# The loop over the tiles beyond the fixed list, at the beginning of an edge pass instead of its end

## The reference

```
def _gnn_layer(edge_index, x, edge_attr, norm, We, be, Wn, bn):
    src, dst = (edge_index[0], edge_index[1])
    parts = [x[src], x[dst]]
    if edge_attr is not None:
        parts.append(edge_attr)
    e = jax.nn.relu(jnp.concatenate(parts, axis=-1) @ We + be)
    msg = e * norm[:, None] if norm is not None else e
    agg = jax.ops.segment_sum(msg, dst, num_segments=x.shape[0])
    x_new = jax.nn.relu(jnp.concatenate([x, agg], axis=-1) @ Wn + bn)
    return (x_new, e)
```

## Time and profile before

| | |
|---|---|
| median of 3 runs | 2377.35 us (2377.28 to 2377.51) |
| the profiled execution | 2376.61 us |
| its span | 2374.4 us |
| mean granted clock of TensorE in it | 0.914 |
| busy: PE, DVE, POOL, ACT | 2020.9, 1455.5, 1063.3, 662.9 us |
| edge pass 0, first POOL gather to node stage | 998.4 to 1412.3 |
| edge pass 1 | 1450.3 to 1884.7 |
| edge pass 2 | 1922.2 to 2335.5 |

### The profile page before, as it was taken

The page is one execution under the profiler, slowest core; times in us unless marked ns, Lnnn a source line. Parts: engine busy times, 40 slices in busy tenths (PEclk is TensorE's granted clock), DMA queues, the critical chain, the costliest instruction groups (busy, mean ns, idle before and its releaser), DMA issues. The chain is left out here.

```text
span 2374.4 us, 50364 instructions
## 1 busy us (share of the span) xinstructions
PE 2020.9 (85%) x14516; PEld 1445.6 (61%) x14516; DVE 1455.5 (61%) x4548; ACT 662.9 (28%) x1344; POOL 1063.3 (45%) x1086
## 2 busy tenths in 40 slices
PE   7687776999999997398888866999999769999983
PEld 4221113454544543287777755999999659888881
DVE  6888873132322323687878846767777467777774
ACT  0145663121211211332333324323233231111111
POOL 0444430000000000377777736777777267777770
PEclk7767767999999998699999978999999889999996
DMA  3022445000000001544444425777777345555541
GB/s 91 14 49 67 87 83 47 0 0 0 0 0 0 0 0 44 209 132 142 143 145 142 144 77 136 210 209 207 209 205 210 93 127 146 146 140 144 142 121 30
DMA packets 188937, 242.83 MB, mean 102 GB/s; under 512 B 53217, under 2 KB 115068, under 8 KB 188076
## 3 DMA queue, kind: packets, MB, share of 16 engines
q1 hardware_dynamic: 155420, 173.31, 25.4%
q0 software_dynamic: 32864, 60.32, 11.1%
q10 hardware_dynamic: 432, 6.29, 0.6%
HBM read 150.92 MB, written 69.26 MB: 93 GB/s over the span
## 5 line engine op out<-in xcount | busy, mean ns | idle before, releaser
L1504 POOL DMA_INDIRECT rows<-p_dram,src_i x912 | 893.0, 979 | 305.1 <-issue 257.4
L1737 DVE TENSOR_TENSOR agg_t<-psum,agg_t 128x128 f32 x1368 | 390.2, 285 | 153.2 <-PE psum L1621 122.9
L1603 PE MATMUL psum<-w_c,before 128*128 128x128 f32 x1824 | 403.6, 303 | 0.0
L1672 ACT ACTIVATE rows<-rows 128x512 f32<-128x512 f32 x228 | 143.7, 630 | 754.6 <-DVE rows L1730 750.5
L884 PE MATMUL psum<-adj,parts 128*128 (+2 forms) x1750 | 339.7, 351 | 5.6 <-ACT agg L963 4.4
L1721 DVE TENSOR_SCALAR hot_w<-col_f,dst_loc,weight 128x128 f32<-128x128 f32 x912 | 319.1, 354 | 0.3
L664 PE MATMUL psum<-src_hot,dst_hot 128*128 128x391 f16 x586 | 228.0, 432 | 81.3 <-ACT psum L686 27.5
L1603 PEld LDWEIGHTS psum<-w_c,before 128*128 128x128 f32 x1824 | 279.7, 194 | 0.0
L1264 POOL MEMSET agg_t<- 128x3200 f32 x1 | 2.8, 2766 | 606.5 <-POOLq L1020 606.5
L1621 PE MATMUL psum<-hot_w,rows 128*128 128x128 f32 x1824 | 247.3, 279 | 29.8 <-ACT rows L1672 25.8
L884 PEld LDWEIGHTS psum<-adj,parts 128*128 128x128 f16 x1750 | 153.0, 98 | 191.1 <-issue 23.4
(11 more groups left out here) (249 smaller groups left out, 2504.3 us busy)
## 6 DMA issues: line engine op xcount, KB each, us to landing
e_dram<-after SPq DMA_DIRECT2D x228, 256.0 KB
before<-e_dram SPq DMA_DIRECT2D x228, 256.0 KB
adj<-stage SPq DMA_DIRECT2D x196, 97.8 KB, 3.5
pair_rows<-sorted_rows SPq DMA_DIRECT2D x114, 128.0 KB, 4.3
rows<-p_dram,src_i POOLq DMA_INDIRECT x912
hot_all<-dst_rows SPq DMA_DIRECT2D x1, 3584.0 KB, 12.5
hot_all<-dst_rows ACTq DMA_DIRECT2D x1, 3072.0 KB, 17.3
hot_all<-dst_rows ACTq DMA_DIRECT2D x1, 2048.0 KB, 10.5
```

The costliest lines, as they stand in the source:

```text
L1504: nc.gpsimd.indirect_dma_start(out=rows[:, b % ROWS, m * D:(m + 1) * D], out_offset=None, in_=p_dram, in_offset=bass.IndirectOffsetOnAxis( ...
L1603: mm = nc.tensor.matmul(o, before[:, q % BEFORE, m * P:(m + 1) * P], w_c[:], start=False, stop=True)
L1672: nc.scalar.activation(e_of(q), source, ACT.Relu).then_inc(e_on, 1)
L1737: nc.vector.tensor_tensor(a, psum[:, A_BANKS[q % len(A_BANKS)], m * P:(m + 1) * P], a, ALU.add).then_inc(agg_on, 1)
```

## The change

The loop's code moves on every engine to the beginning of the pass. On DVE it comes behind the first pair and the twelve `hot_w` operations of the first three slots; on POOL, PE and ACT it comes first. On SP it comes behind the first loads and ahead of the next weights. The loop gets six buffers of its own. The first tile's records are loaded as the pass's first DMA, those of a following tile at the end of a round (so one load more than there are tiles). The sum's product goes to the last of the banks of A_BANKS, for which PE waits at the third slot until the first ordinary sum has been taken (`agg_on`). The waits ahead of the loop are gone.

```
-        over_row = rows[:, 0, 0:D]
-        over_hot = rows[:, 0, P:2 * P]
-        over_hot_w = rows[:, 0, 2 * P:3 * P]
-        over_turned = rows[:, 0, 3 * P:3 * P + P // 2].bitcast(BF16)
-        over_in = before[:, 0, 0:P]
-        over_out = after[:, 0, 0:P]
+        over_row = sb("over_row", [P, D], F32)[:]
+        over_hot = sb("over_hot", [P, P], F32)[:]
+        over_hot_w = sb("over_hot_w", [P, P], F32)[:]
+        over_turned = sb("over_turned", [P, P], BF16)[:]
+        over_in = sb("over_in", [P, P], F32)[:]
+        over_out = sb("over_out", [P, P], F32)[:]
...
         @block.gpsimd
         def _(pool):
+            with pool.Fori(0, overflow(mybir.EngineType.Pool)) as i:
+                pool.wait_ge(over_hots_on, i * 4 + 4)
+                pool.sem_inc(over_gathering, 1)
+                nc.gpsimd.indirect_dma_start(
+                    out=over_row, out_offset=None, in_=p_dram,
+                    in_offset=bass.IndirectOffsetOnAxis(ap=over_src[:].bitcast(U32), axis=0),
+                ).then_inc(over_row_in, 16)
             for b in range(REST_QUADS):
...
         @block.sync
...
+            sp.dma_start(over_rec[:], keep["records"][SORT_TILES * P:(SORT_TILES + 1) * P, :]).then_inc(over_rec_in, 16)
             for i in range(LOADED):
                 load_pair(i)
             if e_before is not None:
                 sp.dma_start(w_c[:], Wc).then_inc(w_in, 16)
                 for q in range(BEFORE):
                     load_before(q)
+            with sp.Fori(0, overflow(mybir.EngineType.SP)) as i:
+                if over_before is not None:
+                    sp.dma_start(over_in, over_before[bass.ds(i, 1), :, :].rearrange("a p n -> (a p) n")
+                                 ).then_inc(over_before_in, 16)
+                if over_after is not None:
+                    sp.wait_ge(over_after_on, i + 1)
+                    sp.dma_start(over_after[bass.ds(i, 1), :, :].rearrange("a p n -> (a p) n"), over_out
+                                 ).then_inc(over_stored, 16)
+                    sp.wait_ge(over_stored, i * 16 + 16)
+                sp.wait_ge(over_agg_on, i + 1)
+                sp.dma_start(over_rec[:], keep["records"][bass.ds(i * P + (SORT_TILES + 1) * P, P), :]
+                             ).then_inc(over_rec_in, 16)
+                sp.wait_ge(over_rec_in, i * 16 + 32)
+                sp.sem_inc(over_kept, 1)
             for to, dram in next_loads:
                 sp.dma_start(to, dram).then_inc(next_in, 16)
...
-            sp.wait_ge(summed, SLOTS)
-            with sp.Fori(0, overflow(mybir.EngineType.SP)) as i:
...
         @block.tensor
...
                 pe.wait_ge(hot_on, (q + 1) * QUAD)
+                if q == len(A_BANKS) - 1:
+                    pe.wait_ge(agg_on, 1)
...
-            for q in range(SLOTS):
-                if q % 3 == 0:
-                    values = lists(q // 3, 0, mybir.EngineType.PE)
-                products(q, values)
-                if q >= LAG:
-                    turn_and_sum(q - LAG)
-            for q in range(SLOTS - LAG, SLOTS):
-                turn_and_sum(q)
-
-            if e_after is not None:
-                pe.wait_ge(after_on, SLOTS)
-            pe.wait_ge(agg_on, SLOTS * QUAD)
             with pe.Fori(0, overflow(mybir.EngineType.PE)) as i:
                 pe.wait_ge(over_hots_on, i * 4 + 4)
...
-                nc.tensor.matmul(psum[:, A_BANKS[0], 0:P], over_row, over_hot_w, start=True, stop=True
+                nc.tensor.matmul(psum[:, A_BANKS[-1], 0:P], over_row, over_hot_w, start=True, stop=True
                                  ).then_inc(over_summed, 1)
+
+            for q in range(SLOTS):
+                if q % 3 == 0:
+                    values = lists(q // 3, 0, mybir.EngineType.PE)
+                products(q, values)
...
         @block.vector
...
             for q in range(LAG + 1):
                 for m in range(QUAD):
                     weighted_hot(q, m)
+            with dve.Fori(0, overflow(mybir.EngineType.DVE)) as i:
+                dve.wait_ge(over_rec_in, i * 16 + 16)
+                nc.vector.tensor_copy(over_src[:], over_rec[:, 3:4]).then_inc(over_hots_on, 1)
...
+                nc.vector.tensor_tensor(a, psum[:, A_BANKS[-1], 0:P], a, ALU.add).then_inc(over_agg_on, 1)
+                dve.wait_ge(over_agg_on, i + 1)
...
-            dve.wait_ge(agg_on, SLOTS * QUAD)
-            dve.sem_inc(over_agg_on, 1)
-            with dve.Fori(0, overflow(mybir.EngineType.DVE)) as i:
```

More of the change, by code:

```diff
@@ L1507, in _ @@
                     ).then_inc(rows_in[b % ROWS], 16)
[L1508 to L1514, removed]
         @block.sync
@@ L1554, in _ @@
                     sp.wait_ge(stored[j], 16 * len(range(j, SLOTS, AFTER)))
-            sp.wait_ge(summed, SLOTS)
-            with sp.Fori(0, overflow(mybir.EngineType.SP)) as i:
[L1557 to L1565, removed]
-                                 ).then_inc(over_stored, 16)
-                    sp.wait_ge(over_stored, i * 16 + 16)
-                    sp.sem_inc(over_kept, 1)
         @block.tensor
@@ L1654, in _ @@
                     nc.tensor.transpose(psum[:, T_BANKS[1], 0:P], over_row, keep["ident"][:])
-                nc.tensor.matmul(psum[:, A_BANKS[0], 0:P], over_row, over_hot_w, start=True, stop=True
+                nc.tensor.matmul(psum[:, A_BANKS[-1], 0:P], over_row, over_hot_w, start=True, stop=True
                                  ).then_inc(over_summed, 1)
+            for q in range(SLOTS):
+                if q % 3 == 0:
+                    values = lists(q // 3, 0, mybir.EngineType.PE)
+                products(q, values)
+                if q >= LAG:
+                    turn_and_sum(q - LAG)
+            for q in range(SLOTS - LAG, SLOTS):
+                turn_and_sum(q)
         @block.scalar
@@ L1679, in take @@
                                      ACT.Copy).then_inc(after_on, 1)
-            for q in range(SLOTS):
-                relu(q)
-                if e_after is not None and q >= LAG:
-                    take(q - LAG)
-            if e_after is not None:
-                for q in range(SLOTS - LAG, SLOTS):
-                    take(q)
             with act.Fori(0, overflow(mybir.EngineType.Activation)) as i:
@@ L1695, in _ @@
                     nc.scalar.activation(over_out, psum[:, T_BANKS[1], 0:P], ACT.Copy).then_inc(over_after_on, 1)
+            for q in range(SLOTS):
+                relu(q)
+                if e_after is not None and q >= LAG:
+                    take(q - LAG)
+            if e_after is not None:
+                for q in range(SLOTS - LAG, SLOTS):
+                    take(q)
         @block.vector
@@ L1746, in _ @@
                     weighted_hot(q, m)
+            with dve.Fori(0, overflow(mybir.EngineType.DVE)) as i:
+                dve.wait_ge(over_rec_in, i * 16 + 16)
+                nc.vector.tensor_copy(over_src[:], over_rec[:, 3:4]).then_inc(over_hots_on, 1)
+                nc.vector.tensor_copy(over_win[:], over_rec[0:1, 4:5]).then_inc(over_hots_on, 1)
+                nc.vector.tensor_scalar(over_hot, keep["col_f"][:], over_rec[:, 1:2], None,
+                                        ALU.is_equal).then_inc(over_hots_on, 1)
+                nc.vector.tensor_scalar(over_hot_w, keep["col_f"][:], over_rec[:, 1:2], over_rec[:, 2:3],
+                                        ALU.is_equal, ALU.mult).then_inc(over_hots_on, 1)
+                dve.wait_ge(over_hots_on, i * 4 + 4)
+                dve.wait_ge(over_row_in, i * 16 + 16)
+                dve.wait_ge(over_spread, i + 1)
+                nc.vector.tensor_tensor(over_row, psum[:, E_BANKS[0], 0:D], over_row, ALU.add
+                                        ).then_inc(over_added, 1)
+                window = over_window(mybir.EngineType.DVE)
+                dve.wait_ge(over_summed, i + 1)
+                a = t["agg_t"][:, bass.ds(window * P, P)]
+                nc.vector.tensor_tensor(a, psum[:, A_BANKS[-1], 0:P], a, ALU.add).then_inc(over_agg_on, 1)
+                dve.wait_ge(over_agg_on, i + 1)
             for q in range(SLOTS):
```

16 lines of the change are left out of this document (removed).

## The result

The changed kernel takes 2371.88 us (median of 20 runs, 2368.26 to 2378.42) against 2377.92 us for the kernel before in the same job (20 runs, 2373.88 to 2381.62). The ratio is 0.9978, 95% interval 0.9971 to 0.9984: 5.2 us less, 3.8 to 6.9 (the ratio is not that of the two medians, which lie 6.0 apart). The forecast was 7.0 us less and 2370.4 us, so it has the size about right and lies just outside that interval. The profiled execution took 2370.53 us (before: 2376.61), with a span of 2368.7 (2374.4).

What follows compares the result with a forecast made beforehand. GpSimd's gathers were taken to pace passes 0 and 2, TensorE pass 1, and a drain to release the node stage. 36.5 off, 30.7 on (net -5.8) and 1.2 for the clock made -7.0: 2370.4 us, range 2364.5 to 2377.0.

Steps and rivals of the forecast that it cites:

- What held the node stage: End of each pass: GpSimd's drain, ending 8.0 us after the last gather, releases the node stage, not the loop's sum or store.
- The tails, 36.5 off: Ends of the three passes: without the loop the node stage starts 12.2, 12.2 and 12.1 us earlier, 36.5 in all.
- The heads, 30.7 on: Starts of the three passes: the loop there delays passes 0, 1 and 2 by 12.8, 8.6 and 9.3 us.
- The upper bound of 35: Pass starts: most they could cost, with 0.8 for the count, eight gathers at 10.7 and SyncE's 2 all paid.
- H: Pass start on VectorE: end of the four operations making the loop's hots, put at 1012.6, 1458.0 and 1930.8 us.
- Between the ends: Middle of each pass: a late ninth gather, or late TensorE in pass 1, comes out at the end in full.
- SyncE's queue, 0.4 us: Pass 1: load_before(3), queued behind SyncE's new waits, goes out late and costs 0.4 us, between 0 and 2.
- The clock, 1.2 us: Node stages: a shorter TensorE pause lets part of the higher clock return, 1.2 us less, at most 8.4.
- (1): Rival, node stages: TensorE's clock stays high there, -14.2 us at most, -12 if one warms late, 2365 us; 12%.
- (3): Rival, pass starts: the loop's gather lands late, sharing DMA engines with other loads, slower, 2383.3 us; 8%.
- (2): Rival, pass starts: each costs 1.3 us more, from TensorE's narrow cover and the count's load, 2374.4 us; 24%.
- (4): Rival: the loop's body isn't reached, or another end holds the node stage as long; 4%, half no change, half slower.

Runs made afterwards that it cites:

- eleven_more: Changed kernel with eleven more gathers at the end of GpSimd's part of each pass: 2412.83 us in one run, against 2372.33 for the changed kernel.
- after_c: The changed kernel unchanged, measured again in the fourth job, TensorE not held back: 2372.33 us, 0.9972 of the kernel before.
- pool_first8: Changed kernel with the first eight ordinary gathers of each pass issued ahead of GpSimd's loop: 1.0002 of the kernel before, TensorE held back.
- after_again: The changed kernel unchanged, measured in the first job, where TensorE was held back: 0.9973 of the kernel before.
- between_one: Changed kernel with the first loop tile's steps between the first three slots, no loop for further tiles: 0.9898 and 0.9890 of the kernel before.
- tail_own: Kernel before with the loop still at the pass's end, but own buffers and its first record loaded ahead: 1.0009 of the kernel before.
- between_slots: Changed kernel with the first loop tile's steps between the first three slots, a loop for further tiles left at the end: 1.0073 of the kernel before.

## Why the prediction was right, step by step

**What held the node stage.** Right, and shown by `eleven_more`: GpSimd's drain. Its end lies 8.0 us behind the last gather in the kernel before, 7.9 in the changed one.

**The tails, 36.5 off.** From the last ordinary gather to the node stage the passes are shorter by 12.26, 12.27 and 12.2, 36.7 in all, forecast 12.2, 12.2, 12.1. The node stage starts 0.33 us behind the last sum (0.4 forecast), and no drain is behind VectorE's.

**The heads, 30.7 on.** The upper bound of 35 adds up to 35.7 by its own terms; nothing hangs on it. By the engine named for each pass they came out at 12.1 (12.8 forecast), 8.15 + 1.0 (8.2 + 0.4) and 8.1 (9.3): 29.4. The parts that were right: the loop's gather 0.8 to 0.9 us behind H (0.79), the first ordinary one H + 2.1 to 2.2 (2.04), eight gathers 10.4, 10.5 and 10.5 (10.1 and 10.3), products at H + 6.9 to 7.1 (7.0). The count's load, costed at nothing, cost nothing: the loop's hots begin at 1012.56, without a gap behind the twelve hot_w. The part that was wrong was H. I let it come 0.3 and 0.4 us later for the record's issue in passes 0 and 2; in fact the pair rows were there sooner after their issue. In pass 2 VectorE could start on them 4.5 us behind their issue in the kernel before and 3.0 in the changed one. H was 1.1 and 1.4 us better than reckoned in passes 0 and 2, and to a tenth as reckoned in pass 1. The profile of `after_c` has the loop's gather at the same distance (14.9, 9.1, 8.7 against 14.7, 9.2, 8.7), so this is no chance of one run. In pass 0 the record has a reason that I had overlooked: before, GpSimd's first eight gathers go out while the pair rows are on their way; now they wait for H. `pool_first8` puts them ahead again, and there VectorE starts on the rows 9.46 us behind their issue, against 8.48 in `after_again` of the same job, 8.47 in the first profile and 9.66 before (one profile each). In pass 2 the same two runs have 4.16 and 3.73, so there most of the 1.5 us stays open.

**Between the ends.** I carried a late ninth gather to the end in full. From the ninth to the last gather it was 377.4 and 377.3 us in pass 0. In pass 2 it was 378.8 and 380.8: two more, with no wait in them (2.0 us of longer gathers). In pass 1 it was 396.6 and 398.0, of which 1.0 is the wait for load_before(3). The 2.4 us beyond that wait ate the 2.5 that H gave back. **That the passes' net, -4.9, came so near to my -5.8 is in part luck:** two errors of some 2.5 us, which no run ties to each other, cancelled. In `after_c` the net is only -2.7, since pass 1 paid 2.7 us more for SyncE's queue.

**SyncE's queue, 0.4 us.** The mechanism was right, the size was not: 1.0 us in one profile and 3.7 in the other, outside the bound of 2. Beside H this is the term of the heads that was mis-sized. The term took 4.3 us for the landing, from a tile that took under 6; it took 4.9 and 6.7.

**The clock, 1.2 us.** The stages behind passes 0 and 1 were 1.5 and 2.1 us shorter and the last one 1.0 longer. For the first six us of the node stages behind passes 0 and 1, this is the view of busy times and granted clock, kernel before and then changed kernel (stretch, length, busy us of PE, PEld, DVE, ACT, POOL with their instructions, clock, DMA share, GB/s):

```profile
1412.00:1418.00 6.00, 5.73 (x7) 2.53 (x8) 0.00 (x0) 0.69 (x1) 0.00 (x0) 0.51 0.00 0
1884.70:1890.70 6.00, 5.99 (x10) 2.78 (x11) 0.00 (x0) 0.90 (x2) 0.00 (x0) 0.65 0.00 0
```

```profile
1413.80:1419.80 6.00, 6.00 (x13) 3.10 (x14) 0.00 (x0) 1.41 (x3) 0.00 (x0) 0.76 0.00 0
1882.20:1888.20 6.00, 5.96 (x16) 3.15 (x17) 0.76 (x2) 1.76 (x3) 0.00 (x0) 1.00 0.01 3
```

and in `after_c`, the same code:

```profile
1414.80:1420.80 6.00, 5.99 (x7) 2.51 (x8) 0.00 (x0) 0.69 (x1) 0.00 (x0) 0.50 0.00 0
1887.60:1893.60 6.00, 6.00 (x12) 2.90 (x13) 0.00 (x0) 1.29 (x2) 0.00 (x0) 0.72 0.01 3
```

Behind pass 1 the 2.4 GHz level held throughout in the first profile; in the second the clock was 0.50 and 0.72, as low as before the change, and these stages were 37.35 and 36.38 us long against 37.31 and 36.77 before. The last stage took 38.9, 39.9 and 38.9 us with 0.67, 0.50 and 0.67 in its first six. At each of the three places the higher clock goes with the shorter stage in the three profiles, which is why I put the difference down to the clock; no run changed the clock alone. So it gave 2.6 us in one execution and 0.4 in the other. A gain that belongs to the change can't be claimed from this; it belongs to the spread of the runs.

**The rivals.** (1), the clock high at the node stages, happened behind one pass of two in one profile and not in the other. (3), the late landing, did not happen: 3.6, 3.7 and 3.8 us, as in the tails before (3.8, 3.5 and 3.5; the earlier trace rows). The Trainium skill, DMA: Bandwidth & Descriptors, "Latency and other measured facts", would have made it 1.8 us more at high load; the trace does not agree for this gather. The two landings of load_before(3), 4.9 and 6.7 us, do lie 1.8 apart, but no run shows that the memory's load was the reason. (2), heads dearer by 1.3 us each, is what pass 1 of `after_c` looks like, by SyncE's queue and not by the count's load. (4) did not happen: the loop's gather stands at each head, and no other drain came to hold the node stage as long.

## What to carry to other kernels

Before moving a loop whose count is known only at run time, ask whether its body has work to do and whether it runs at a count of 0: here it did, and without it the kernel took 37 us less than before (21 to 54, with TensorE held back), against 5 to 7 for the move. A test of the count ahead of the loop was not tried. Before a piece of work is moved off the end of a block, look at what the last instruction of each queue waits for there: here a queue's drain 8 us behind its last gather held the node stage longer than the loop's own chain did, and with the gather ahead of all the others no gather stands late enough for its drain to be the last (it ends 1.6 us ahead of VectorE's in pass 0). A short chain over five engines put at the start of a block is paid by every engine that stands in it, at the latency of the whole chain; laid between steps that run anyway, it cost 0.6 to 1.7 us a head here. And where a moved step sits ahead of a queue of loads, reckon the landing with the longest such load of that stretch in the profile, not the middle one.

## What the runs showed of the hardware

- GpSimd's drain at the end of a block ends long after its last indirect gather has landed: 7.3 to 7.4 us behind the gather's end in `pool_first8` and `between_one`, 7.9 in the changed kernel, 8.0 with the loop last in the kernel before and in `tail_own` (7.3 in `between_slots`), 8.3 and 8.8 with five and eleven gathers more. The landing itself took 2.4 to 3.3 us from the issue for those eleven. It is not the number of gathers alone, since `pool_first8` has as many as the changed kernel. What the drain waits for stays open.
- In three jobs all kernels ran 18% longer, with matmuls one every 0.7 us in stretches, nothing in the profile that releases them, and a granted clock of 0.79 where it was 1.00. One of these jobs and the last one, at 2378 us, ran on the same chip. The loops ahead of pass 0 took 999 us as ever; only the passes grew. The cause stays open.
- A loop of this kind executes its body once though its count leaves nothing to do: from 0 and, in `between_slots`, from 1, with a count of 0.
